# Gated cross-attention block with an FFN: queries from a tile turned on the host, a second buffer for the moved values of half 0, later reciprocals of half 1, and transfers in another order

## The reference

```python
x = x + tanh(g_xattn) * xattn(layernorm(x), ctx, pos, pos, Wq, Wkv, Wout, bout)
x = x + tanh(g_ffn) * ffn(layernorm(x), gate_w, up_w, down_w, expert_weight, gamma, beta)

# xattn: ctx is (16, 256, 256)
q = x @ Wq ; k, v = split(ctx @ Wkv)          # 32 heads of 16
q, k = axial_rope(q, pos), axial_rope(k, pos) # angles from two coordinates
attn = softmax(q k^T / 4) v
return attn @ Wout + bout

# ffn: INTER = 2048, 8 experts, top 2
scale = sum of the two largest of (x @ gate_w)
y = relu(x @ up_w)^2 @ down_w + (x @ expert_weight) * scale
return layernorm(y) * gamma + beta
```

## Time and profile before

| | |
|---|---|
| median of 3 runs | 1636.23 us (1629.36 to 1639.9) |
| the profiled execution | 1626.67 us, span 1624.9 us |
| TensorE (PE) busy | 1530.4 us, 94% |
| VectorE (DVE) busy | 985.7 us, 61% |
| ScalarE (ACT) busy | 640.3 us, 39% |
| GpSimd (POOL) busy | 338.1 us, 21% |
| opening | to about 44 us |
| attention, rounds -1 to 15 | about 44 to 785 us |
| FFN | about 785 to 1625 us |

### The profile page before, as it was taken

One profiled execution on the slowest core, in us unless ns is written; L12 is line 12 of the kernel. 1 busy time (PEld: TensorE's weight loads), 2 busy tenths in 40 slices (PEclk: granted clock), 3 DMA queues, 4 the chain that ended last, 5 costly groups with the idle time before them and its releaser, 6 DMA issues.

```text
span 1624.9 us, 25920 instructions
## 1 busy us (share of the span) xinstructions
PE 1530.4 (94%) x9498; PEld 1132.6 (70%) x9498; DVE 985.7 (61%) x1416; ACT 640.3 (39%) x962; POOL 338.1 (21%) x406
## 2 busy tenths in 40 slices
PE   8789999999999999984999999999999999999997
PEld 6456565666666666552688887887878888788886
DVE  7787887788888778753663543535435354253524
ACT  4355555555556555543542222222222222222221
POOL 5322232333222332211100201102101021010202
PEclk9799999999999999976999999999999999999999
DMA  6645454555555555433450110101101011010101
GB/s 174 135 90 127 121 134 121 134 124 138 137 122 123 129 127 123 113 83 107 118 157 20 46 33 13 46 20 46 33 7 53 20 46 33 1 52 26 39 14 40
DMA packets 80623, 131.11 MB, mean 81 GB/s; under 512 B 21624, under 2 KB 35064, under 8 KB 80504
## 3 DMA queue, kind: packets, MB, share of 16 engines
q1 hardware_dynamic: 80504, 129.48, 31.2%
HBM read 51.17 MB, written 16.78 MB: 42 GB/s over the span
## 4 chain that ended last, share of the span: by engine, by line
PE 65%; SPq 13%; DVE 12%; DMA 3%; issue 3%; POOL 2%; ACT 1%; DVEq 0%; POOLq 0%; ACTq 0%
PE pP L1095 12%; PE pA L1296 11%; PE pB L1296 11%; PE pO L1095 10%; PE pT L1095 8%; SPq L540 7%; DVE mneg L1516 5%; PE pA L1193 3%; PE pO L1221 3%; SPq L577 2%; DMA den<-av_s 2%; SPq L568 2%; PE pM L1102 2%; PE pP L1102 2%; PE pM L1095 2%
## 5 line engine op out<-in xcount | busy, mean ns | idle before, releaser
L1516 DVE TENSOR_REDUCE mneg<-pA 128x4 f32<-128x1024 f32 x250 | 305.8, 1223 | 114.0 <-PE pA L1193 111.5
L994 ACT ACTIVATE probs<-pB 128x1024 f32<-128x1024 f32 x249 | 255.3, 1025 | 228.3 <-PE pB L1209 218.8
L794 POOL TENSOR_SCALAR var_eps<-meanvar 128x1 f32<-128x1 f32 x96 | 34.5, 360 | 994.4 <-DVE meanvar L1398 994.3
L1619 DVE TENSOR_TENSOR relu<-relu 128x512 f32<-128x512 f32 x128 | 88.4, 690 | 252.1 <-ACT hid L1048 252.1
L1296 PE MATMUL pA<-dn,hid 128*128 128x512 f32 x768 | 198.0, 393 | 1.7 <-DVE hid L1621 1.5
L1296 PE MATMUL pB<-dn,hid 128*128 128x512 f32 x768 | 195.6, 390 | 0.0
L1095 PE MATMUL pP<-fT,up 128*128 128x512 f32 x768 | 188.5, 394 | 0.0
L1095 PE MATMUL pO<-fT,up 128*128 128x512 f32 x768 | 184.8, 389 | 0.0
L1296 PEld LDWEIGHTS pA<-dn,hid 128*128 128x128 f32 x768 | 143.4, 188 | 34.5 <-DVE hid L1621 5.1
L1296 PEld LDWEIGHTS pB<-dn,hid 128*128 128x128 f32 x768 | 144.8, 189 | 30.3
L1095 PEld LDWEIGHTS pO<-fT,up 128*128 128x128 f32 x768 | 144.0, 188 | 30.5 <-issue 0.4
(11 more groups left out here) (200 smaller groups left out, 2004.3 us busy)
## 6 DMA issues: line engine op xcount, KB each, us to landing
stk<-kT SPq DMA_DIRECT2D x180, 128.0 KB, 2.9
stq<-qT SPq DMA_DIRECT2D x180, 128.0 KB, 3.0
fres<-x_scratch SPq DMA_DIRECT2D x34, 256.0 KB, 2.8
xin<-x SPq DMA_DIRECT2D x32, 256.0 KB, 3.3
numer<-av_s SPq DMA_DIRECT2D x128, 64.0 KB, 2.4
xres<-x SPq DMA_DIRECT2D x32, 256.0 KB, 2.9
x_scratch<-xres SPq DMA_DIRECT2D x32, 256.0 KB, 2.1
out<-y_s SPq DMA_DIRECT2D x32, 256.0 KB, 2.0
```

Of the source, the lines that this page charges most:

```text
L994: nc.scalar.activation(probs[:, s % 4, :, :, :].rearrange("p a b s -> p a (b s)"), psum[:, :, :], ACT.Exp).then_inc(exp_done, 1)
L1516: nc.vector.tensor_reduce(mneg[par][:, :, 2 * u:2 * u + 2].rearrange("p t q -> p q t"), psum[:, :, :].rearrange("p q (t k) -> p q t k", t= ...
L1619: nc.vector.tensor_tensor(r[:], r[:], r[:], ALU.mult).then_inc(sq_made, 1)
```

## The change

1. Queries. x is handed over a second time, turned in tiles by the host (`xT`). For batches 2 to 15 jobs X0 and X1 and `ln_apply` are gone. SP loads the turned raw tile into `xn`, GpSimd splits it into high part and rest (`split_x`, two instructions of 128x512). The mean is taken out by centring Wq: TensorE computes the column means of Wq once after the opening (eight products), ScalarE copies them, the four chunks of Wq are loaded again and GpSimd centres and splits them (`centre_weights`, twelve instructions). The deviation is applied by scaling the tile's rows of the cosine and sine tables on VectorE (two instructions of 128x32 before each rotation of Q). The two tiles of a batch get an inverse deviation each (`rstds`).
2. `numer` and `aT_lo` are now a tile per half, and half 0 has two of each, by the batch's parity. `move_av` of half 0 is issued in the batch's own round, behind `gather_den(i, 0)`.
3. Reciprocals of half 1 go from step 3 to step 5, b1 from step 6 to step 8, `round_av` of half 1 from step 8 to 9, O0's first half from step 9 to 10.
4. SP: `scatter_recips` of half 1 behind the maxima and the residuals; in round 15 the four tiles first, the denominators ahead of the weights, the small tables last. GpSimd's first two inverse deviations of the FFN stand ahead of the residual sums.

```diff
 SCHEDULE = {
-    0: ("X0",),
+    0: (),
...
-    5: ("X1", "kT0"),
-    6: ("b1",),
+    5: ("kT0",),
+    6: (),
     7: ("K1", "Q1<"),
-    8: ("Q1",),
-    9: ("kT1", "O0<"),
-    10: ("qT0",),
+    8: ("Q1", "b1"),
+    9: ("kT1",),
+    10: ("qT0", "O0<"),
...
-RECIPROCALS = {14: 0, 3: 1}
-ROUNDED = {4: 0, 8: 1}
+RECIPROCALS = {14: 0, 5: 1}
+ROUNDED = {4: 0, 9: 1}
...
+            def load_xT(b, t):
+                if (b, t) == (2, 0):
+                    sp.wait_ge(*done_of("X1", 1))
+                else:
+                    sp.wait_ge(xT_split, 2 * (split_no(b, t) - 1))
+                alone(sp)
+                sp.dma_start(xn[:], xT[b * TT + t]).then_inc(xT_in, INC)
...
             def move_av(b, h):
                 sp.wait_ge(av_taken, GROUPS * b + GROUPS // 2 * (h + 1))
-                if some(b):
-                    sp.wait_ge(done[BANK["O1"]], number("O1", b - 1))
+                last = b - 1 if h else b - 2
+                if last >= 0:
+                    sp.wait_ge(done[BANK["O1"]], number("O1", last))
...
-                if within(bt):
-                    move_av(bt, 0)
-                if ending:
-                    first_loads()
                 if within(b1) and not opened("kT1", b1):
                     load_stack(b1, (par + 1) % 2, 1, "k")
+                if within(b2):
+                    load_xT(b2, 1)
+                if ending:
+                    first_tiles()
                 if within(bt):
                     gather_den(bt, 1)
                 if within(bt - 1):
                     store_x1(bt - 1, 1)
+                if ending:
+                    for key in ffn_chunks[:4]:
+                        load_w(key)
                 if within(bt):
                     move_av(bt, 1)
-                    scatter_recips(bt, 1)
                 if within(i):
                     load_max(i, par % 2, 1)
                 if within(bt):
                     load_residual(bt)
+                    scatter_recips(bt, 1)
...
+                if ending:
+                    first_rest()
                 gather_den(i, 0)
+                move_av(i, 0)
...
+            def split_x(b, t):
+                n = split_no(b, t)
+                used, of = ("Q0", b) if t else ("Q1", b - 1)
+                pool.wait_ge(*done_of(used, of))
+                pool.wait_ge(xT_in, INC * n)
+                alone(pool)
+                xv = xn[:].rearrange("p (c s) -> p c s", c=KC)
+                nc.gpsimd.tensor_copy(xnT[0][:], xv).then_inc(xT_split, 1)
+                pool.wait_ge(xT_split, 2 * n - 1)
+                nc.gpsimd.tensor_tensor(xnT[1][:], xv, xnT[0][:].bitcast(F32), ALU.subtract).then_inc(xT_split, 1)
+
+            def centre_weights():
+
+                pool.wait_ge(col_made, 1)
+                for c in range(KC):
+                    pool.wait_ge(w_again[c], INC)
+                    nc.gpsimd.tensor_tensor(raw_again[c], raw_again[c], col_mean, ALU.subtract).then_inc(centred, 1)
...
                 if prepares:
                     rope_sum(b2, "Q0")
+                    split_x(b2, 1)
+                ending = isinstance(i, int) and i == B - 1
+                if ending:
+                    for u in range(2):
+                        inv_std(NT + u + 1)
...
+                        if i == 0 and s in (0, 3):
+                            act.wait_ge(centred, 3 * 2 if s == 0 else 3 * KC)
...
+            act.wait_ge(col_done, 1)
+            nc.scalar.copy(col_mean, pO[:, :]).then_inc(col_made, 1)
             later_setup()
...
+                    if name[0] == "Q" and not opened(name, b):
+                        dve.wait_ge(rstd_made, n + 1)
+                        dve.wait_ge(*taken_of(f"K{t}", b))
+                        alone(dve)
+                        for side in (cos_t, sin_t):
+                            own = side[:, n, :, :, :].rearrange("p w k l -> p (w k l)")
+                            nc.vector.tensor_scalar(own, own, rstds[t][:, 0:1], None, ALU.mult).then_inc(scaled, 1)
+                        dve.wait_ge(scaled, 2 * split_no(b, t))
```

116 lines of the change are left out of this document (78 added, 38 removed), and 4 rows, old and new, of tables (BANK, LAG).

## The result

The kernel after takes 1588.92 us (median of 4 executions, 1585.79 to 1590.04), the kernel before beside it 1636.01 us (4 executions, 1629.36 to 1639.9). The ratio is 0.9713, 95% interval 0.9678 to 0.9749: 47 us less, where 28 were forecast. A ratio is worked out on the executions of two kernels side by side; where a kernel scatters it differs a little from the quotient of the medians. The profiled execution of after took 1587.83 us, its span is 1586.0.

A forecast was written before the change was run, and what follows sets the result against it. TensorE, busy 94% of the span, was taken as the bound. Terms -7 - 6.5 - 15.1 - 1.5 + 2.4 sum to -28 us: 1599 for the profiled execution, 1608 beside the median, range 1590 to 1631.

The forecast's parts named there:

- The regular batch: Each of 14 batches: gross gain 3.1 us less 1.5 and 1.15 of costs, -0.45 us, about -7 in all.
- The reciprocals at step 5: VectorE's denominator subtraction races GpSimd's: loss 0.6 us if served first, 1.7 if not; half and half, +1.15 per batch.
- Thin steps: Steps 0, 5 and 9, left with little TensorE work, wait, and ScalarE's rounding holds an exponential: +1.5 us per batch.
- The second buffer: SP's queue: moving half 0 earlier and loading turned tiles costed at nothing, covered by b1 asking about 5 us later.
- (b): Rival: VectorE never caught and clock falls go, -15 instead of -7 and -3 in the regular batches: 1597 us, chance 0.15.
- Round 14: Steps 4 to 11 shrink from 26.4 us to 18.5 as denominators come sooner; -7.9 worked out, -6.5 taken.
- End of attention: Stop before the first FFN transpose: inverse deviation no longer behind residual sums, transpose starts near 743.0, -15.1 us.
- Behind the stop: After the stop before the FFN: TensorE at 1.2 GHz for less time, half 0's move off SP's queue; -1.5 us for both.
- Opening: Before the first maximum: ScalarE's gates wait for the column-mean products, 1.7 us, and the copy, 0.6: +2.4 us.
- (a): Rival: GpSimd wins the subtraction every time, regular batches gain nothing: 1615 us, 1620 with occasional clock falls, chance 0.22.
- (c): Rival: the stop in step 6 drops TensorE's clock in every batch, +32 us against -21: 1647 us, chance 0.06.
- (d): Rival: the end of attention keeps half its stop, tiles and weights sharing SP's queue: -20, 1616 us, chance 0.12.

The follow-up runs named there:

- late_by_three: The kernel after with three small VectorE reductions between the rounding of half 1's denominators and their subtraction: 1613.5 us, ratio to before 0.9845.
- x_on_tensor: The kernel after with the queries' input turned on TensorE again, without turned copy, centring and table scaling: 1589.7 us, ratio to before 0.9712.
- recips_at_3: The kernel after with the third part of the change undone, half 1's reciprocals back in step 3: 1604.3 us, ratio to before 0.9828.
- recips_at_5_alone: The kernel before with only the third part of the change, half 1's reciprocals in step 5: 1603.3 us, ratio to before 0.9815.
- stack_behind: scale_early with the stack of kT issued behind the reciprocals in every round, the turned tile still ahead of the denominators: 1645.3 us, ratio to before 1.0079.
- dens_first: scale_early with half 1's denominators ahead of the turned tile in SP's queue, and in round 14 ahead of the kT stack: 1576.1 us, ratio to before 0.9653.
- scale_early: recips_at_3 with Q0's two tables scaled on VectorE right behind the reciprocals in step 3: 1589.5 us, ratio to before 0.9712.
- late_by_reading: The kernel after with one small VectorE reduction between the rounding of half 1's denominators and their subtraction: 1590.5 us, ratio to before 0.9719.
- end_order_alone: The kernel before with only the change's orders of round 15 (numer stays a tile per half): 1620.2 us, ratio to before 0.9873.

## Why the prediction was wrong, point by point

The direction was right, and so was the mechanism of most places; the time came out 19 us below the forecast and 1 us below the range. By the stages of the profiled executions the regular part brought some 14 us more than its term and the opening cost 1 less, while the stretch behind round 13's kT1 brought 3 less and the FFN took 1 more; another 8 us lie in the step from the profiled execution to the median. The terms:

- **The regular batch, -0.45 us: this is the step that failed.** It measured -1.57 (20.3 us in 13 batches). Two costs of the sum were too high, by about the same.
- **The reciprocals at step 5, +1.15 ("I take it half and half").** VectorE wins the race in every batch, so the term is 0.6 and not 1.15; late_by_three shows that its upper bound, 1.7, is what a lost race costs.
- **Thin steps, +1.5.** The waits of the earlier trace rows are gone as said, and what is left, 15.3 us in ten batches, looks like the forecast 1.5. But it holds the stop behind the reciprocals (0.62), which the sum charges under their own term. So the thin steps cost 0.9: the waits in steps 5 and 9 measured 0.49 and 0.41 against 0.5 to 0.6 each, and the 0.15 of step 0 and the 0.25 behind ScalarE did not come. With 0.6 and 0.9 the batch is 44.8 - 3.1 + 1.5 = 43.2, as measured.
- **The second buffer, "at nothing".** The 1.08 us of X's transposes were in the gross gain; x_on_tensor shows that 0.8 of them fill waits that open without them. The sum for the batch allowed for that, but it did not ask which part of the change then makes the gain. It is that the denominators are no longer late. With X on TensorE the second buffer's earlier moves do it, or the later step, each enough in a regular batch: the moves are worth at most 3 us with the third part there and 27 to 35 without it. With the turned tile in SP's queue the moves are not enough: recips_at_3 has them, and takes 1604.3. The cover that the text named for the cost is there, but the gain was not counted. Quiet batches of before take 43.5 to 44.4 us, so about half of the 1.6 us per batch is the disturbed ones. They were in the mean of 44.8, but the text gave their end to rival (b) alone.
- **The step to the median.** The forecast multiplied the profile's 1599 by 1636.23/1626.67. That takes the excess of the other executions for a constant share. It was the long batches: in before their sum differs by 20 us between two profiles, after, whose executions lie within 4 us of each other, has none. Of the 47 us, 39 show between the two profiled executions, and 8 are this. Without the factor the forecast would have been 1599.
- **Round 14, -6.5:** 26.4 to 18.46 is -7.9, the sum that the prediction had worked out before it took less.
- **End of attention, -15.1:** 18.72 to 3.44 is -15.3, by rest 0 and the deviation behind it as named. The third part counts too: recips_at_5_alone shortens the stop to 15.38 with the old orders. How it does is not shown.
- **Behind the stop, -1.5:** this term had the wrong sign. The clock was to be low for less time after a shorter stop; it was low for longer (0.52 against 0.61 in 16 us), and the part up to the FFN took 1.7 us more.
- **Opening, +2.4:** +1.6 at the first maximum, by the named chain.
- **The rivals:** (a) is refuted by the 0.22 us. (b) is the case that happened, VectorE's subtraction never caught and the falls of the clock in the regular batches gone, but for 3 us at 97 in the first; its 1597 holds the same factor, without which it is 1588. (c) did not happen in after, but stack_behind and recips_at_3 show its mechanism: 4.7 to 6 us per batch where the clock fell, and 1.7 where it did not, instead of the 2.3 that was priced. The 2.1 us from which it was to decide is no sharp point. Four of late_by_three's thirteen stops of 1.76 took the clock down, and so did one of 1.32 in dens_first and one in scale_early, while two of 2.25 and 2.31 in recips_at_3 did not. (d) is refuted by the stop of 3.44.

What stays open: which engine is served first when both ask within some 0.02 us, and which of several equal stops of 1.3 to 2.3 us takes the clock down.

## What to carry to other kernels

Where executions of one kernel scatter by over 1% and one profile shows a few long intervals among equal ones, count those intervals as part of the time to win: take the difference from the quiet interval, look at the granted clock behind each stop, and don't scale a profile to the median by a factor. When several parts of a change relieve the same late transfer, they don't add up: run each alone and each left out before one is called the gain. Small VectorE instructions on SBUF want a place where GpSimd is idle by more than the scatter of its start, and moving one of them moves the others.

## What had not been expected of the hardware

- When VectorE's rounding had waited for GpSimd's copy, VectorE's next subtraction was served first in all 13 batches (0.22 us, GpSimd's 1.35 instead of 1.28), and so it was in late_by_reading, where GpSimd's started 0.02 us earlier by the profile. With a lead of 0.27 us for GpSimd it took 1.08, and in end_order_alone, where its rounding had not waited, 1.34 with a lead of 0.01.
- Stops of the same length had different prices. In recips_at_3 four of six stops of 2.11 to 2.31 us were followed by a granted clock of 0.50 to 0.66 in the next 10 us and batches 4.7 to 6 us above a quiet one, the other two by a clock of 1.00 and 1.7 us. Of the four stops of 1.32 us in scale_early and dens_first two took the clock down and two did not.
- In the 16 us behind the transpose that ends a stop of 3.44 us the granted clock was 0.52, behind one of 18.72 us it was 0.61: the shorter stop did not make the stretch at 1.2 GHz shorter.
